# Attention's 74-row column tail: three part products packed into two

## The reference

```python
h = layernorm(x) @ W
e = leaky_relu(h @ a1 + (h @ a2).T, 0.2)
attention = softmax(where(adj > 0, e, -9e15), axis=1)
x = x + relu(attention @ h)            # the product that the change touches
y = layernorm(x)
idx = argmax(y @ Wr + br)              # one expert a row, at most C-1 rows an expert
x = x + gate**2 * (relu(y @ W1[idx] + b1[idx]) @ W2[idx]) + gate * b2[idx]   # rows placed by rank
```

## Time and profile before

| | us |
|---|---|
| median of 3 runs | 265.61 (265.56 to 267.66) |
| profiled execution, device time | 263.48 |
| its span | 261.7 |
| TensorE busy | 250.5 |
| VectorE busy | 180.9 |
| ScalarE busy | 128.6 |
| GpSimd busy | 90.1 |
| granted TensorE clock | 0.998 of 2.4 GHz |

### The profile page before, as it was taken

How to read it: one execution, slowest core, us unless ns; L and a number is a source line. 1 busy time by engine, 2 the same in 40 slices (tenths; PEclk the granted TensorE clock), 3 DMA queues, 4 the chain that set the end, 5 groups by cost and what they waited for, 6 DMA issues and landing times.

```text
span 261.7 us, 4579 instructions
## 1 busy us (share of the span) xinstructions
PE 250.5 (96%) x1649; PEld 210.8 (81%) x1649; DVE 180.9 (69%) x429; ACT 128.6 (49%) x263; POOL 90.1 (34%) x113
## 2 busy tenths in 40 slices
PE   6799989999999999999999999999999999999990
PEld 1489989988888778778778889899977968879780
DVE  3988768996978977785762573847296685856931
ACT  2737786853765475555553121342447155454330
POOL 4334891000341432112120224118253834841502
PEclk9999999999999999999999999999999999999999
DMA  6990000320488888421211213136978679888001
GB/s 189 375 318 32 1 5 0 106 81 27 159 210 284 273 262 248 168 79 40 80 42 41 82 39 96 52 117 176 353 237 294 247 258 290 283 293 285 12 7 44
DMA packets 19210, 40.47 MB, mean 155 GB/s; under 512 B 2810, under 2 KB 3130, under 8 KB 19188
## 3 DMA queue, kind: packets, MB, share of 16 engines
q1 hardware_dynamic: 16196, 34.17, 39.5%
q0 software_dynamic: 2176, 4.80, 6.1%
q10 hardware_dynamic: 816, 1.21, 1.5%
HBM read 32.93 MB, written 8.31 MB: 158 GB/s over the span
## 4 chain that ended last, share of the span: by engine, by line
PE 87%; POOL 3%; DVE 2%; DMA 2%; issue 2%; ACT 2%; POOLq 1%; ACTq 0%
PE bank L1426 30%; PE bank L1690 12%; PE bank L1728 7%; PE bank L1364 6%; PE bank L1412 5%; PE bank L1756 5%; PE bank L1441 3%; PE bank L1660 2%; PE bank L1346 2%; DMA w_raw<-in_L_gnn_W_dram 2%; PE bank L1676 2%; PE bank L1703 2%; PE bank L1453 2%; PE bank L1464 2%; PE bank L1560 1%
## 5 line engine op out<-in xcount | busy, mean ns | idle before, releaser
L1426 PE MATMUL bank<-h_hi,pt_lo 128*128 128x512 f32 (+1 forms) x110 | 45.9, 417 | 0.0
L1426 PE MATMUL bank<-h_lo,pt_hi 128*128 128x512 f32 (+1 forms) x110 | 43.6, 396 | 0.0
L1426 PE MATMUL bank<-h_hi,pt_hi 128*128 128x512 f32 (+1 forms) x110 | 43.4, 394 | 0.0
L411 POOL TENSOR_TENSOR x_all<-x_all,w_raw 128x512 f32<-128x512 f32 x10 | 18.1, 1810 | 65.2 <-ACT w_raw L589 65.2
L1690 PE MATMUL bank<-prob,w 128*128 128x168 f32 x224 | 33.2, 306 | 0.0
L1690 PEld LDWEIGHTS bank<-prob,w 128*128 128x128 f32 x224 | 32.6, 189 | 0.7 <-issue 0.2
L754 ACT ACTIVATE adj_s<-bank,b_cols 128x168 f32<-128x168 f32 x28 | 11.3, 402 | 33.6 <-PE bank L1690 33.6
L1426 PEld LDWEIGHTS bank<-h_hi,pt_hi 128*128 128x128 f32 (+1 forms) x110 | 20.7, 188 | 4.9
L1426 PEld LDWEIGHTS bank<-h_hi,pt_lo 128*128 128x128 f32 (+1 forms) x110 | 20.7, 188 | 3.8
L1426 PEld LDWEIGHTS bank<-h_lo,pt_hi 128*128 128x128 f32 (+1 forms) x110 | 20.8, 189 | 3.6
L611 ACT ACTIVATE wide<-adj_s,off_b 128x1354 f32<-128x1354 f32 (+1 forms) x11 | 15.8, 1432 | 14.1 <-DVE off_b L887 14.1
(11 more groups left out here) (203 smaller groups left out, 558.1 us busy)
## 6 DMA issues: line engine op xcount, KB each, us to landing
w<-in_L_ffn_W_dram SPq DMA_DIRECT2D x16, 1024.0 KB, 6.7
adj_s<-in_adj_dram SPq DMA_DIRECT2D x10, 677.0 KB, 5.3
x_rows<-x_all SPq DMA_DIRECT2D x10, 257.0 KB, 3.2
out_dram<-x_all SPq DMA_DIRECT2D x10, 256.0 KB
x_all<-in_x_dram SPq DMA_DIRECT2D x9, 256.0 KB, 5.6
prob<-in_L_ffn_b_dram SPq DMA_DIRECT2D x5, 256.0 KB, 7.2
w_raw<-in_L_gnn_W_dram ACTq DMA_DIRECT2D x4, 256.0 KB, 5.5
adj_s<-in_L_ffn_b_dram SPq DMA_DIRECT2D x2, 256.0 KB, 7.0
```

What stands on the lines that cost most here:

```text
L411: pool.tensor_tensor(x_all[0:R, t, 0:D], x_all[0:R, t, 0:D], relu_s[0:R, :], ALU.add).then_inc(s_x1, 1)
L1426: ins = pe.matmul(o_ps[par][0:R, :], p[0:K, par, k, 0:R], h[0:K, k, :], start=(k == 0 and n == 0), stop=(k == NT - 1 and n == 2))
```

## The change

Only column tile 10, the one with 74 rows, is treated anew. Write its rows as A (the first 64, `TA`) and B (the last 10, `TB`). The three part products are packed into two by placing row copies in the 128 rows of the contraction:

- product 1, 128 rows: `pt_lo` x `h_lo`, where rows 0 to 63 of the two tiles now hold low p and *high* h of A, and rows 64 to 127 *high* p and low h of A;
- product 2, 94 rows (`TD` = 64 + 3 x 10) of `pt_hi` x `h_hi`: rows 0 to 63 high p and high h of A, and three copies of B: low p x high h, high p x low h, high p x high h.

To have three copies of B, a second exp of 20 columns writes two more copies of B's weights behind `prob` (which grows to N + 20 columns), so that `p_turn` transposes 94 columns for this tile; and the x tile 10 is transposed with B's columns repeated three times (`x_high`, `x_low`: two instructions each for one), so that h tile 10 comes out with 94 rows. `h_high(10)` makes four copies for two. `h_low(10)` makes, for each half, one subtraction and two further instructions, which put the low part of h into the middle copy of B by a mask column `is_lo`. GpSimd makes the mask in four instructions (`low_rows`), placed between `power(8)` and `f2_product(6)`; the constants' counts rise by four. In the loop, `p_high` has one more copy a row tile and `p_low` one more subtraction. Four small tiles (`gate_s`, `emp`, `dest`, `src`) move into `first` to make room. `attend` and `attend_last` run two products for column tile 10.

```diff
+    TA = P // 2
+    TB = TAIL - TA
+    TD = TA + 3 * TB
+    NP = N + 2 * TB
...
-        prob = sb("prob", [P, 2, N])
+        prob = sb("prob", [P, 2, NP])
...
+            def low_rows():
+                pool.memset(is_lo[:, 0:1], 1.0).then_inc(s_const, 1)
+                pool.wait_ge(s_const, 11)
+                pool.affine_select(out=is_lo[:, 0:1], in_=is_lo[:, 0:1], compare_op=ALU.is_ge, fill=0.0,
+                                   base=-(TA + TB), pattern=[[0, 1]], channel_multiplier=1).then_inc(s_const, 1)
+                pool.wait_ge(s_const, 12)
+                pool.affine_select(out=is_lo[:, 0:1], in_=is_lo[:, 0:1], compare_op=ALU.is_ge, fill=0.0,
+                                   base=TA + 2 * TB - 1, pattern=[[0, 1]], channel_multiplier=-1).then_inc(s_const, 1)
+                pool.wait_ge(s_const, 13)
+                pool.tensor_scalar(is_lo[:, 1:2], is_lo[:, 0:1], -2.0, 1.0, ALU.mult, ALU.add).then_inc(s_const, 1)
...
             for t in range(NT - 2):
                 power(t)
+            low_rows()
             f2_product(FCOL)
             f2_product(FCOL + 1)
...
+                    if t == NT - 1:
+                        act.activation(xt_hi[:, par, :, 0:TA], src_[:, :, 0:TA], ACT.Copy)
+                        act.activation(xt_hi[:, par, :, TA:TD].rearrange("p c (r n) -> p c r n", r=3),
+                                       src_[:, :, TA:TAIL].unsqueeze(2).broadcast_to([P, KC, 3, TB]), ACT.Copy
+                                       ).then_inc(s_xhi, 1)
...
             def h_high(t):
-                R, par = rows(t), t % 2
+                R, par = (rows(t) if t < NT - 1 else TD), t % 2
                 act.wait_ge(s_h, t + 1)
                 for j in range(2):
+                    if t == NT - 1:
+                        act.activation(h_lo[0:TA, t, j * H0:(j + 1) * H0], h_ps[par][j][0:TA, 0:H0], ACT.Copy)
                     ins = act.activation(h_hi[0:R, t, j * H0:(j + 1) * H0], h_ps[par][j][0:R, 0:H0], ACT.Copy)
...
-                    act.activation(pt_hi[0:TAIL, par, k1 - 1, 0:R], v[0:TAIL, k1 - k0 - 1, 0:R], ACT.Copy
+                    act.activation(pt_hi[0:TD, par, k1 - 1, 0:R], v[0:TD, k1 - k0 - 1, 0:R], ACT.Copy)
+                    act.activation(pt_lo[TA:P, par, k1 - 1, 0:R], v[0:TA, k1 - k0 - 1, 0:R], ACT.Copy
                                    ).then_inc(s_phi[b], 1)
...
-                act.activation(prob[0:R, par, :], arg[t % 3][0:R, :], ACT.Exp,
+                act.activation(prob[0:R, par, N:NP].rearrange("p (r n) -> p r n", r=2),
+                               arg[t % 3][0:R, N - TB:N].unsqueeze(1).broadcast_to([R, 2, TB]), ACT.Exp)
+                act.activation(prob[0:R, par, 0:N], arg[t % 3][0:R, :], ACT.Exp,
                                accum_out=rsum[0:R, par, :]).then_inc(s_prob, 1)
...
+                    if t == NT - 1:
+                        dve.tensor_tensor(h_lo[TA:P, t, c], h_ps[par][j][0:TA, 0:H0], h_hi[0:TA, t, c].bitcast(F32),
+                                          ALU.subtract)
+                        dve.tensor_scalar(h_pick[TA:TD, c], h_ps[par][j][TA:TD, 0:H0], is_lo[TA:TD, 0:1], None, ALU.mult
+                                          ).then_inc(s_step, 1)
+                        dve.wait_ge(s_step, j + 1)
+                        dve.scalar_tensor_tensor(h_hi[TA:TD, t, c], h_hi[TA:TD, t, c].bitcast(F32), is_lo[TA:TD, 1:2],
+                                                 h_pick[TA:TD, c], ALU.mult, ALU.add)
...
-                    dve.tensor_tensor(pt_lo[0:TAIL, par, k1 - 1, 0:R], v[0:TAIL, k1 - k0 - 1, 0:R],
-                                      pt_hi[0:TAIL, par, k1 - 1, 0:R].bitcast(F32), ALU.subtract
+                    dve.tensor_tensor(pt_lo[0:TA, par, k1 - 1, 0:R], v[0:TA, k1 - k0 - 1, 0:R],
+                                      pt_hi[0:TA, par, k1 - 1, 0:R].bitcast(F32), ALU.subtract)
+                    dve.tensor_tensor(pt_hi[TA:TAIL, par, k1 - 1, 0:R], v[TA:TAIL, k1 - k0 - 1, 0:R],
+                                      pt_hi[TA:TAIL, par, k1 - 1, 0:R].bitcast(F32), ALU.subtract
                                       ).then_inc(s_plo[b], 1)
...
-                    K = rows(k)
+                    K = rows(k) if k < NT - 1 else TD
...
+            def terms(k):
+                if k == NT - 1:
+                    return (P, pt_lo, h_lo), (TD, pt_hi, h_hi)
+                return (P, pt_lo, h_hi), (P, pt_hi, h_lo), (P, pt_hi, h_hi)
...
-                    K = rows(k)
-                    for n, (p, h) in enumerate(((pt_lo, h_hi), (pt_hi, h_lo), (pt_hi, h_hi))):
+                    for n, (K, p, h) in enumerate(terms(k)):
                         ins = pe.matmul(o_ps[par][0:R, :], p[0:K, par, k, 0:R], h[0:K, k, :],
-                                        start=(k == 0 and n == 0), stop=(k == NT - 1 and n == 2))
+                                        start=(k == 0 and n == 0), stop=(k == NT - 1 and n == 1))
```

45 lines of the change are left out of this document (28 added, 17 removed).

## The result

The changed kernel takes 271.84 us (median of 6 runs, 271.13 to 276.34); the kernel before, on the same chip, 265.51 us (6 runs). The ratio is 1.028, with a 95% interval of 1.022 to 1.033. Medians are over all executions; ratios leave out executions more than 1.5% above the fastest of the same kernel. The time lies far above the predicted range of 264.2 to 266.6 us.

What follows compares the result with a forecast made beforehand. TensorE was taken as the bound. Removed products -2.58, low_rows +1.08, start of attention +0.95 and dispatch(0) +0.33 summed to -0.22 us: 265.4 us against a median of 265.61, range 264.2 to 266.6.

Steps and rivals of the forecast that it cites:

- an addition is costed at nothing: In the loop, the added ScalarE and VectorE instructions were to fit within a 9.80 us period: cost 0.
- The overlap of consecutive instructions (0.08 us): Pricing of added instructions: consecutive instructions of one engine were taken to overlap by about 0.08 us.
- its price: At row tile 10 of h, VectorE's h_low(10) was to take 2.50 us against 0.66 before, 1.84 more.

Runs made afterwards that it cites:

- e14: Changed kernel with ScalarE's 64-row copy taken from pt_hi behind its residual part and VectorE's argument ahead of the 10-row subtraction; 265.75 us, ratio 1.002.
- e7: Changed kernel with low_rows earlier, residual addition held for the argument, h_low(10)'s selection on ScalarE and GpSimd, exp_below(0) ahead of the last p_high; 265.36 us.

## What to carry to other kernels

Before an addition is costed at nothing, follow the ring of waits that it joins, once round, and compare its length with the bound engine's period: a busy sum cannot show it, and idle time in the ring is not slack. Where VectorE and GpSimd run big SBUF instructions side by side, look at which starts first and by how much (0.08 us here): that margin is a resource, and one short instruction spends it. If it is spent, change the order before taking out the work.

## What the runs showed of the chip

The overlap of consecutive instructions (0.08 us) is not always there. Timeline of VectorE in the changed kernel, `h_low(10)`, which in the earlier trace rows was two subtractions that step by about 0.33 us:

```profile
58.10 1.63 DVE L943 SCALAR_TENSOR_TENSOR adj_s<-adj_s,off_a,wide 128x1354 f32<-128x1354 f32 x1
59.76 0.42 DVE L848 TENSOR_TENSOR h_lo<-bank,h_hi 64x256 fp32r<-64x256 f32 x1
60.19 0.48 DVE L850 TENSOR_SCALAR w_raw<-bank,is_lo 30x256 f32<-30x256 f32 x1
60.71 0.48 DVE L853 SCALAR_TENSOR_TENSOR h_hi<-h_hi,is_lo,w_raw 30x256 fp32r<-30x256 f32 x1
61.20 0.42 DVE L848 TENSOR_TENSOR h_lo<-bank,h_hi 64x256 fp32r<-64x256 f32 x1
```

59.76 + 0.42 = 60.18, and the next starts at 60.19; in the earlier trace rows 61.32 + 0.69 = 62.01 stands against a start at 61.93. The overlap is missing where what an instruction reads or writes starts on another partition (0 or 64) than in the instruction ahead of it, in the loop too (81.37 + 0.29 = 81.66 in e14's rows, where the next starts at 81.69), and it is there between two of the same kind: in e7 the two subtractions that write from partition 64 stand next to each other and take 0.75 us together.

```profile
54.88 0.75 DVE L860 TENSOR_TENSOR h_lo<-bank,h_hi 64x256 fp32r<-64x256 f32 x2 [0.41 <-ACT w_raw L540]
```

It cost some 0.1 us at each such change, which makes most of the 0.50 us that `h_low(10)` took over its price (2.34 for 1.84). This is not the whole rule: in the changed kernel the overlap is missing behind the argument too (114.34 + 2.53 = 116.87, the next starts at 116.91), where both instructions work from partition 0 and the one ahead of the argument did not. In the kernel before, 76.15 + 1.61 = 77.76 stands against a start at 77.68 at the same place. No run tried the start partition by itself, so the cause stays open.
